# Fetching the queries of the first attention one batch later, from another queue, and the maxima in four pieces

## The reference

```python
Q = query @ Wq + bq                      # 32 heads of 16 numbers
K = key @ Wk + bk                        # 8 key heads, each serves 4 query heads
V = value @ Wv + bv
scores = jnp.einsum('bhgqd,bhkd->bhgqk', Q, K) * scale
w = jax.nn.softmax(scores, axis=-1)
y = jnp.einsum('bhgqk,bhkd->bhgqd', w, V)
...
x = x + _L0_xattn_ref(_layernorm(x, axis=-1), ctx_4096, ctx_4096, ...)
x = x + _L0_ffn_ref(_layernorm(x, axis=-1), ...)      # 16 experts, 4 for each token
x = x + _L1_xattn_ref(_layernorm(x, axis=-1), ctx_4096, ...)
x = x + _L1_ffn_ref(_layernorm(x, axis=-1), ...)
```

## Time and profile before

| | us |
|---|---|
| median of 3 runs (1247.02 to 1248.53) | 1247.69 |
| the profiled execution | 1247.02 |
| its span, first to last instruction | 1245.6 |
| PE busy | 1192.0 (96%) |
| DVE busy | 816.7 (66%) |
| ACT busy | 672.6 (54%) |
| POOL busy | 410.2 (33%) |

### The profile page before, as it was taken

The page is one execution under the profiler, slowest core; times in us unless marked ns, Lnnn a source line. Parts: engine busy times, 40 slices in busy tenths (PEclk is TensorE's granted clock), DMA queues, the critical chain, the costliest instruction groups (busy, mean ns, idle before and its releaser), DMA issues.

```text
span 1245.6 us, 16579 instructions
## 1 busy us (share of the span) xinstructions
PE 1192.0 (96%) x5948; PEld 920.3 (74%) x5948; DVE 816.7 (66%) x1541; ACT 672.6 (54%) x1562; POOL 410.2 (33%) x491
## 2 busy tenths in 40 slices
PE   8989889999999999899999999999999999999997
PEld 5646446667776667688888888877888888888765
DVE  4468857677766784756665667764466566676857
ACT  2245633377777785355545555653455555656621
POOL 3511321577777782012222322320023232232200
PEclk9899989999999999899999999999999999999999
DMA  8674312695679776321121221211212121121101
GB/s 288 176 181 118 139 55 77 250 281 102 118 191 293 151 144 127 138 75 60 43 68 43 68 60 60 68 52 43 77 43 66 45 65 64 60 60 34 59 1 67
DMA packets 72913, 127.93 MB, mean 103 GB/s; under 512 B 12216, under 2 KB 31544, under 8 KB 70136
## 3 DMA queue, kind: packets, MB, share of 16 engines
q1 hardware_dynamic: 53024, 73.90, 19.5%
q0 software_dynamic: 18448, 50.36, 16.3%
q10 hardware_dynamic: 1360, 2.62, 0.5%
HBM read 150.37 MB, written 26.48 MB: 142 GB/s over the span
## 4 chain that ended last, share of the span: by engine, by line
PE 73%; DVE 8%; POOL 6%; issue 6%; DMA 3%; ACT 3%; SPq 1%; ACTq 0%; POOLq 0%; DVEq 0%
PE bank L466 54%; PE bank L1982 7%; PE bank L1958 4%; POOL moe L1577 3%; PE bank L683 2%; POOL xs L1566 2%; PE bank L697 2%; PE bank L649 1%; PE bank L2297 1%; DMA wf_raw<-in_wffn,weight_row 1%; PE bank L664 1%; DMA x<-in_x 1%; PE bank L1253 1%; POOL wf_raw L1556 1%; DVE mx L873 1%
## 5 line engine op out<-in xcount | busy, mean ns | idle before, releaser
L1950 POOL TENSOR_SCALAR p<-p,mx 128x256 f32<-128x256 f32 x256 | 163.3, 654 | 521.8 <-DVE mx L1944 521.8
L1160 DVE TENSOR_TENSOR wf_lo<-wf_raw,wf_hi 128x512 fp32r<-128x512 f32 x188 | 121.6, 689 | 36.2 <-ACT wf_hi L1154 34.1
L1936 ACT ACTIVATE p<-bank,mx 128x256 f32<-128x256 f32 x256 | 118.0, 485 | 10.7 <-DVE mx L1926 10.6
L466 PE MATMUL bank<-xnA_hi,w1q_hi 128*128 128x512 f32 x288 | 118.9, 413 | 3.6 <-DVE xnA_lo L460 3.2
L1154 ACT ACTIVATE wf_hi<-wf_raw 128x512 fp32r<-128x512 f32 x192 | 110.2, 626 | 12.2 <-DMA wf_raw<-in_wffn,weight_row 12.2
L466 PE MATMUL bank<-xnA_hi,w1q_lo 128*128 128x512 f32 x288 | 115.1, 400 | 0.0
L466 PE MATMUL bank<-xnA_lo,w1q_hi 128*128 128x512 f32 x288 | 114.4, 397 | 0.0
L1965 ACT ACTIVATE p1T_hi<-bank 128x512 fp32r<-128x512 f32 x128 | 75.1, 596 | 65.7 <-PE bank L1958 65.7
L1890 ACT ACTIVATE q1T_hi<-bank 128x512 fp32r<-128x512 f32 x64 | 38.2, 597 | 132.4 <-PE bank L466 132.4
L466 PE MATMUL bank<-w1o_hi,a1T_hi 128*128 128x512 f32 x256 | 105.2, 411 | 0.1
L1896 DVE TENSOR_TENSOR q1T_lo<-bank,q1T_hi 128x512 fp32r<-128x512 f32 x64 | 44.2, 690 | 93.2 <-ACT q1T_hi L1890 93.2
(11 more groups left out here) (335 smaller groups left out, 2975.7 us busy)
## 6 DMA issues: line engine op xcount, KB each, us to landing
w_raw<-in_wq SPq DMA_DIRECT2D x64, 256.0 KB, 2.7
w_raw<-in_wo SPq DMA_DIRECT2D x64, 256.0 KB, 2.7
moe<-xn SPq DMA_DIRECT2D x2, 2304.0 KB, 11.7
returned<-moe SPq DMA_DIRECT2D x8, 512.0 KB, 6.4
q0st<-q_rows SPq DMA_DIRECT2D x14, 256.0 KB, 4.7
x<-in_x SPq DMA_DIRECT2D x8, 256.0 KB, 6.1
ctx<-in_ctxT SPq DMA_DIRECT2D x2, 1024.0 KB, 10.3
k0bd<-k_rows SPq DMA_DIRECT2D x16, 128.0 KB, 2.4
```

The costliest lines, as they stand in the source:

```text
L466: ins = nc.tensor.matmul(ps, a, b, start=(n == 0), stop=(n == len(pairs) - 1))
L1160: nc.vector.tensor_tensor(wf[m % 2][1][:, a, c, :], raw[m % STREAMS][:, a, c, :], wf[m % 2][0][:, a, c, :].bitcast(F32), ALU.subtract).the ...
L1936: ins = nc.scalar.activation(pr1[s % 2][:, h, :], banks.of(("s1", s, n))[:, hh * 2 * P:(hh + 1) * 2 * P], ACT.Exp, bias=m[:, UH + h:UH + h ...
L1950: ins = nc.gpsimd.tensor_scalar(pr1[s % 2][:, h, :], pr1[s % 2][:, h, :], m[:, 3 * UH + h:3 * UH + h + 1], 1.0, ALU.mult, ALU.mult)
```

## The change

- Fetching: in the loop on SP the queries fetched at batch b are those of b + 2, right behind the keys of b + 2, and the loop begins at batch 2. The gate and expert loads follow batch 2.
- The second half's queries are written to `q_rows` by SP instead of POOL, before the loop. They count on the four semaphores of the first half's writes.
- The maxima: `m0T` is laid out as 32 partitions with hi and lo side by side (before: 64 partitions, hi above lo). One DMA of 64 rows into 4 rows becomes four DMAs of 16 rows into 1 row. For batch 0, ACT issues two of the four.
- The semaphore `zeroed` is split into `kbd_set` and `vp_set`; each wait asks for the same clearings as before.

```diff
-        mT = [sb(f"m0T{i}", [2 * H0, P], F32R) for i in range(2)]
+        mT = [sb(f"m0T{i}", [H0, 2, P], F32R) for i in range(2)]
...
-        def maxima_in(queue, b):
-            queue.dma_start(qst[b % RING0][QROWS:QROWS + MROWS, :, :, :].bitcast(F32).rearrange("p k j t -> p (k j) t"),
-                            mT[b % 2][:, :].bitcast(F32)).then_inc(S[f"ld_m0{b % RING0}"], 16)
+        def maxima_in(queue, b, h):
+            half = H0 // 2
+            for q in range(2):
+                row = QROWS + 2 * q + h
+                queue.dma_start(qst[b % RING0][row:row + 1, :, :, :].bitcast(F32).rearrange("p k j t -> p (k j) t"),
+                                mT[b % 2][h * half:(h + 1) * half, q, :].bitcast(F32)).then_inc(
+                                    S[f"ld_m0{b % RING0}"], 16)
...
                 for m in range(blocks.start, blocks.stop):
-                    sp.wait_ge(*((S["st_q_half1"], 32 * KT) if half else (S[f"st_q{m}"], 32)))
+                    sp.wait_ge(S[f"st_q{m}"], 32 * (half + 1))
...
             def maxima(b):
                 sp.wait_ge(S["m0_lo"], b + 1)
-                maxima_in(nc.sync, b)
+                maxima_in(nc.sync, b, 0)
+                if b:
+                    maxima_in(nc.sync, b, 1)
...
             maxima(1)
             keys_in(3)
-            maxima(2)
-            queries_in(4)
-            keys_in(4)
-            queries_in(5)
-            sp.wait_ge(S["wo0_lo"], KT)
-            sp.wait_ge(S["v0"], B)
-            load(gate_raw[:, :, :], A["gate0"]).then_inc(S["ld_gate0"], 16)
-            load(gbias[:, :], A["gbias0"].broadcast_to([P, E0])).then_inc(S["ld_gate0"], 16)
-            load(raw[0][:, :, :, :], A["wffn"][0]).then_inc(S["ld_shared"], 16)
-            for b in range(3, B):
+            for m in range(KT):
+                sp.wait_ge(S["q0_lo"], KT + m + 1)
+                queries_out(nc.sync, 1, m)
+            for b in range(2, B):
                 maxima(b)
                 if b + 2 < B:
                     keys_in(b + 2)
-                if b + 3 < B:
-                    queries_in(b + 3)
+                    queries_in(b + 2)
+                if b == 2:
+                    sp.wait_ge(S["wo0_lo"], KT)
...
+                    load(raw[0][:, :, :, :], A["wffn"][0]).then_inc(S["ld_shared"], 16)
...
                 if j == KV0 - 1:
                     maxima(0)
+                    act.wait_ge(S["m0_lo"], 1)
+                    maxima_in(nc.scalar, 0, 1)
                     nc.scalar.activation(preload[:, :], eps, ACT.Exp)
...
-            for m in range(KT):
-                pool.wait_ge(S["q0_lo"], KT + m + 1)
-                queries_out(nc.gpsimd, 1, m)
             for b in range(2, B):
                 values_spread(b)
```

More of the change, by code:

```diff
@@ L425, in norm_scale @@
             if g in (2, 3):
-                dve.wait_ge(S["zeroed"], KRING + 6)
+                dve.wait_ge(S["vp_set"], 6)
                 if g == 3:
@@ L499, in queries_out @@
                 queue.dma_start(q_rows[half, 4 * m:4 * m + 4, :, c].rearrange("n h d t -> (n h) d t"),
-                                q0T[c][:, m, :].bitcast(F32)).then_inc(S["st_q_half1" if half else f"st_q{m}"], 16)
-        def maxima_in(queue, b):
-            queue.dma_start(qst[b % RING0][QROWS:QROWS + MROWS, :, :, :].bitcast(F32).rearrange("p k j t -> p (k j) t"),
-                            mT[b % 2][:, :].bitcast(F32)).then_inc(S[f"ld_m0{b % RING0}"], 16)
+                                q0T[c][:, m, :].bitcast(F32)).then_inc(S[f"st_q{m}"], 16)
+        def maxima_in(queue, b, h):
[5 more added lines that the diff above has]
+                                    S[f"ld_m0{b % RING0}"], 16)
         def sync_attention0():
@@ L529, in keys_in @@
                 half, tok = b // HB, slice((b % HB) * P, (b % HB + 1) * P)
-                sp.wait_ge(S["zeroed"], b % KRING + 1)
+                sp.wait_ge(S["kbd_set"], b % KRING + 1)
                 sp.wait_ge(S["st_k"], 32 * (half + 1))
@@ L587, in sync_attention0 @@
                     keys_in(b + 2)
-                if b + 3 < B:
-                    queries_in(b + 3)
+                    queries_in(b + 2)
+                if b == 2:
+                    sp.wait_ge(S["wo0_lo"], KT)
+                    sp.wait_ge(S["v0"], B)
+                    load(gate_raw[:, :, :], A["gate0"]).then_inc(S["ld_gate0"], 16)
+                    load(gbias[:, :], A["gbias0"].broadcast_to([P, E0])).then_inc(S["ld_gate0"], 16)
+                    load(raw[0][:, :, :, :], A["wffn"][0]).then_inc(S["ld_shared"], 16)
         VALUES_AT = {KV0 - 1: (HB, HB + 1), KV0: (HB + 2,), KV0 + 1: (HB + 3,)}
@@ L764, in maxima @@
                 if b >= 2:
-                    act.wait_ge(S[f"ld_m0{(b - 2) % RING0}"], 16 * ((b - 2) // RING0 + 1))
-                nc.scalar.activation(mT[b % 2][0:H0, :], banks.of(("m0", b))[0:H0, 0:P], ACT.Copy,
+                    act.wait_ge(S[f"ld_m0{(b - 2) % RING0}"], 64 * ((b - 2) // RING0 + 1))
+                nc.scalar.activation(mT[b % 2][:, 0, :], banks.of(("m0", b))[0:H0, 0:P], ACT.Copy,
                                      scale=-1.0).then_inc(S["m0_hi"], 1)
@@ L880, in maxima @@
                 nc.vector.scalar_tensor_tensor(
-                    out=mT[b % 2][H0:2 * H0, :], in0=banks.of(("m0", b))[0:H0, 0:P], scalar=-1.0,
-                    in1=mT[b % 2][0:H0, :].bitcast(F32), op0=ALU.mult, op1=ALU.subtract).then_inc(S["m0_lo"], 1)
+                    out=mT[b % 2][:, 1, :], in0=banks.of(("m0", b))[0:H0, 0:P], scalar=-1.0,
+                    in1=mT[b % 2][:, 0, :].bitcast(F32), op0=ALU.mult, op1=ALU.subtract).then_inc(S["m0_lo"], 1)
             def divide(b, n):
@@ L1013, in gpsimd_attention0 @@
                                         ALU.subtract).then_inc(S["wo0_lo"], 1)
-            pool.wait_ge(S["zeroed"], KRING + 5)
+            pool.wait_ge(S["vp_set"], 5)
             values_spread(0)
@@ L1024, in gpsimd_attention0 @@
                 if b == B - 2:
-                    pool.wait_ge(S["st_q_half1"], 32 * KT)
-                    nc.gpsimd.memset(zeros, 0.0).then_inc(S["zeroed"], 1)
+                    for m in range(KT):
+                        pool.wait_ge(S[f"st_q{m}"], 64)
+                    nc.gpsimd.memset(zeros, 0.0).then_inc(S["vp_set"], 1)
                 attended(b - 2)
@@ L1077, in sync_experts @@
             load = nc.sync.dma_start
-            sp.wait_ge(S["zeroed"], KRING + 6)
+            sp.wait_ge(S["vp_set"], 6)
             for s in range(2):
```

14 lines of the change are left out of this document (7 added, 7 removed).

## The result

The changed kernel takes 1263.80 us (median of 4 runs, 1257.99 to 1265.64) against 1247.88 (4 runs): ratio 1.012, 95% interval 1.0087 to 1.0153. The profiled execution has 1262.72 us and a span of 1261.2; before it was 1247.02 and 1245.6. The forecast was 1260.5 (range 1251 to 1267), 1.1% over the profiled execution of before.

A forecast was written before the change was run, and what follows sets the result against it. PE was taken as the pace setter, busy 96% of the span. Terms -1.2 (batch 4) + 9.9 (query waits) + 4.4 (half clock) + 0.3 (maxima) = +13.4 us over the profiled 1247.02: forecast 1260.5 us, range 1251 to 1267.

The forecast's parts named there:

- the step that carries the forecast: First scores of batches 5, 6 and 7: PE waits 3.3 us each for queries fetched behind the keys, +9.9 us.
- The eight DMAs: Key and query fetch of batches 5 to 7: 8.8 us from the first key issue to the last landing.
- the other work: PE's work in the loop between a batch's key fetch and the scores using those keys: 5.5 us.
- Rivals 2 and 3: Fetch lands sooner, little shows: 1247.2 us, chance 0.07; the hole at batch 4 goes, faster: 1241.7 us, chance 0.04.
- rival 4: Everything goes long: waits of 5.3 us, each with the dearer half clock; +26.8, 1273.8 us, chance 0.06.
- The clock: Half clock behind the waits of batches 5 and 6: 2.2 us each, +4.4 us, bounds zero and 5.8.
- rival 1: Queries late at batches 5 to 7 but the clock stays up: +5.6, 1252.6 us, chance 0.21.
- Behind batch 7: Half clock of 2.2 us set against 1.9 us of vanishing DVE and POOL waits: nothing, bounds -1.9 and +2.9.
- Batch 4: First scores +0.2 us, even chance of saving the 2.9 us half clock: -1.2 us, bounds -2.7 and +2.2.
- my own signs of being wrong: No PE wait at scores of batches 5 to 7, loop clock 1.00, or longest wait at turned scores for `m0T`.
- The maxima of the later batches: Four pieces land later; the wait could show in batches 6 and 7: 0 to 1.8 us, taken as 0.3.
- Ring order: Descriptors are consumed in order, so loads queued behind cannot slow batch 4's queries; its term would stay at -1.2 us.

The follow-up runs named there:

- Filling the three waits: Changed kernel plus 25 transposes of the identity on PE ahead of the first scores of batches 5, 6 and 7: 1257.74 us against 1261.03 unfilled.
- the last kernel: Kernel before with queries of batch 5 fetched behind the maxima of batch 3, gate and first expert loads behind the keys of batch 3: 1246.57 us.
- three attempts at closing it: Kernel before with queries of batch 5 later (1244.00 us); with the last query block earlier (1255.55); with queries of batch 5 later and expert's load earlier (1246.57).

## Why the prediction was right, and where not

**The cause.** It was forecast that PE waits at the first scores of batches 5, 6 and 7 for queries that now travel with the keys. It does: 2.23, 2.81 and 3.00 us, 8.0 in place of 9.9. This is the step that carries the forecast, and it is right. Two sizes make the difference. The eight DMAs took 8.3, 8.6 and 8.7 us from the first key issue to the scores (109.03 less 100.71, 125.06 less 116.50, 141.19 less 132.54), against 8.8; and the other work up to the wait took 6.1, 5.8 and 5.7 us, against 5.5. The order alone gives +14.5 us, and taking it back gives 8.1. Rivals 2 and 3 are out, and so is rival 4, whose waits would be 5.3 us each.

**The clock.** Forecast 4.4 us behind batches 5 and 6. From the scores to the next key issue it is 116.50 - 109.03 = 7.47 and 132.54 - 125.06 = 7.48 us, against 5.91 before: 1.6 each, 3.1 together. The stretches at half clock there are of the shorter kind (3.2 us, not 6.8). Filling the three waits gave about 3.3 us back. In the profiled execution rival 1, in which the clock stays up, is out, and the term was too dear by 1.3. But the argument against rival 1, that 2.44 us were enough, is weaker than it looked: with the writes back on POOL a wait of 2.84 us left the clock at 1.00. The length of a wait alone doesn't decide it, and a share of what rival 1 describes happens in single executions.

**Behind batch 7.** Counted at nothing, measured +0.1 (15.28 us from the scores to the last maxima before, 15.37 after). The waits for DVE and POOL there went, the half clock came (0.50 in the last of the rows by stretch).

**Batch 4.** This step failed, and it met one of my own signs of being wrong: the longest single wait of PE in this part (5.19 us) is at the turned scores for `m0T`, though the three for the queries are longer together (8.0). I put -1.2 us there and held the maxima of batch 2 for covered: "They are out by about 76, before the maxima at 79.48". They were not. SP needed 0.6 to 1.6 us for each write once some were under way, the last went out at 79.00, and the maxima pieces behind them landed at 86.85. PE waited 5.19 us, and the scores of batch 4 came without a wait of their own at 94.82 instead of 90.49. With the clock at 0.50 from 85.5 to 92.3, the key fetch of batch 5 is late by 100.71 - 99.31 = +1.4 us, 2.6 more than forecast. The writes alone give a maxima wait of 3.7, the pieces alone 1.7; 5.2 for both together. I had worked the issue times from rows of a lightly loaded queue (0.62 us for a write, 2.0 for four pieces; 3.67 was measured) and bounded only the landing.

**The maxima of the later batches.** I took 0.3 us for them. In batch 3 PE waited 0.19 us, and in batch 7 (before 161.29) 0.92; there the next wait, for ACT's exponential, is 2.61 instead of 3.54, which takes it back. So the term is about nothing.

**Sum.** 1.4 at batch 4, 8.0 of waits, 3.1 of half clock, 1.0 of longer other work, 0.1 behind batch 7: 13.6, which is the delay of 13.7 at the last maxima; forecast 13.4. The errors are +2.6 at batch 4, +1.0 for the other work and +0.1 behind batch 7, against -1.9 in the waits, -1.3 in the half clock and -0.3 in the maxima: they cancel to 0.2. That the total is this good is luck; its main term is not.

Of the last 1.9 us up to the span's 15.6, 1.4 arise between 168 and 176, most of them where the clock is at 0.50:

```profile
168.00:174.00 6.00, 6.00 (x23) 3.73 (x24) 0.89 (x3) 3.31 (x9) 0.64 (x1) 0.50 0.86 334
```

Up to 167.74 the delay is still 13.7 (154.04 before). There the clock fell for 6 us and more, where before it fell for 3.4, and the last transposes of the next layer norm come 15.1 us late (180.72 against 165.65). In the second profiled execution of the changed kernel PE had the same 2.61 us of waiting at this place (before 167.78), the granted clock of the same stretch is 1.00, and the same transposes start at 177.84, 2.9 us sooner. So this part can come and go between executions of one kernel.

**Two rules weighed.** With the queries of batch 5 moved away from behind them, the keys of batch 4 took 5.7 us from the last issue (83.41) to the scores instead of 6.4, and 3.3 (90.45 less 87.11) with the expert's load moved too; the queries of batch 4 were ahead in all three. In the last kernel SP's issues were more spread out, which makes 3.3 look better than it is. Counted from the first issue of the eight DMAs it is 10.1 us (80.44 to 90.49), 9.3 (79.79 to 89.08) and 8.1 (82.36 to 90.45). So what lies behind seems to matter here. These are single profiles, so it is no clean proof. Ring order (the Trainium skill, "DMA: Bandwidth & Descriptors", section "Queues, rings and completion order"), by which I took it not to matter, is not borne out by the three.

The smaller pieces did not pay for their three more issues: alone they leave the median where it was. In their profile SP takes 2.72 us to issue the maxima of batch 2, and PE waits 1.69 us:

```profile
79.83 2.72 SPq L506 DMA_DIRECT2D q0st<-m0T  x4
```

Before, one issue took 0.56 us and the wait was 0.22:

```profile
82.35 0.47 PE L664 MATMUL bank<-q0st,k0bd 100*128 100x256 f32 x2 [0.22 <-DMA q0st<-m0T]
```

The rule that a transfer uses the largest number of engines, up to 16, that divides its slowest dimension (the Trainium skill, the same page, section "Why a DMA increments its semaphore by 16 and not by 1") would have made each piece land sooner by 0.4 us, by the prediction's estimate; no run here shows a gain of that size.

## What to carry to other kernels

Two transfers that one consumer needs together should not be queued together just ahead of it: the one that can go a round earlier is what hides the other. Before a queue is given more work, look at what short transfer is queued behind it, since it pays for the whole backlog. And a hole in the timeline may be hiding the next one: two of three attempts at closing it only moved it.

## What was not expected of the hardware

- The issue of a DMA on SP took longer when large ones were under way: 0.6 us for the first three writes of 256 KB, 0.9 to 1.6 for the later ones, and 3.67 us for four pieces of 8 KB right behind them, where 2.40 were enough with no writes ahead. The same writes from POOL took 0.60 to 0.89 us each, but they were spread over 30 us.
- The length of a wait did not settle what the clock did. It fell to 0.50 with idle stretches of 2.23 us (before 109.03) and 2.44 us, and not with those of 1.54 and 1.17 us; but it also stayed at 1.00 behind 2.01 and 2.84 us with the writes back on POOL, and of two executions of the changed kernel that waited 2.61 us at the same place, one fell and one did not. A forecast of such a step should carry both outcomes.
- Four transfers of 16 rows were not better than one of 64 rows: 2.72 us of issue and a wait of 1.69, against 0.56 and 0.22.
